# Fused attention block on one core: another order of stores and loads in stage one, and a separate path for the end of the last pair

## The reference

```python
h = _layernorm(x, axis=-1) * (1 + ca) + sa
x = x + ga * _L0_attn_ref(h, L0_attn_W_attn, L0_attn_W_proj)
h = _layernorm(x, axis=-1) * (1 + cb) + sb
x = x + gb * _L0_ffn_ref(h, ...)          # h @ W.T + b, and h @ (low-rank).T
```

## Time and profile before

| what | value |
|---|---|
| median of 3 runs | 1395.97 us (1394.33 to 1398.8) |
| the profiled execution, its own time | 1395.44 us |
| its span, first to last instruction | 1393.3 us |
| PE busy | 1251.6 us (90%) |
| ACT busy | 1274.1 us (91%) |
| DVE busy | 957.1 us (69%) |
| POOL busy | 194.4 us (14%) |
| last instruction of stage one on SP issued | 142.38 us |
| last exponential done | 1363.57 us |
| last computing instruction done | 1387.01 us |

### The profile page before, as it was taken

How to read it: one execution, slowest core, us unless ns; L and a number is a source line. 1 busy time by engine, 2 the same in 40 slices (tenths; PEclk the granted TensorE clock), 3 DMA queues, 4 the chain that set the end, 5 groups by cost and what they waited for, 6 DMA issues and landing times.

```text
span 1393.3 us, 28816 instructions
## 1 busy us (share of the span) xinstructions
PE 1251.6 (90%) x11067; PEld 742.9 (53%) x11067; DVE 957.1 (69%) x2082; ACT 1274.1 (91%) x2629; POOL 194.4 (14%) x405
## 2 busy tenths in 40 slices
PE   7994899999999999999999999999999988888784
PEld 5552455555555555555555555555555555444442
DVE  4852677777777777777777777777777766656453
ACT  2534899999999999999999999999999999999991
POOL 0323000201103030303011020303030201102030
PEclk9997899999999999999999999999999999999996
DMA  4795711010000001010101000000101010000000
GB/s 152 244 294 190 225 41 28 20 28 20 20 19 15 24 19 28 20 27 21 28 20 28 20 12 24 15 26 21 28 17 27 16 28 16 22 15 12 23 4 13
DMA packets 94447, 64.62 MB, mean 46 GB/s; under 512 B 59595, under 2 KB 89570, under 8 KB 94306
## 3 DMA queue, kind: packets, MB, share of 16 engines
q1 hardware_dynamic: 94306, 62.75, 15.2%
HBM read 41.74 MB, written 20.97 MB: 45 GB/s over the span
## 4 chain that ended last, share of the span: by engine, by line
PE 36%; ACT 34%; DVE 7%; issue 6%; ACTq 0%; DVEq 0%
ACT fast_s_ps L1087 21%; PE fast_s_ps L866 16%; ACT fast_probs L1087 12%; PE fast_t_ps L923 6%; PE fast_t_ps L892 5%; PE fast_t_ps L908 4%; DVE fast_negmax L1146 3%; PE fast_t_ps L954 2%; DVE fast_probsT L1165 2%; PE fast_s_ps L875 1%; PE fast_t_ps L934 1%; DVE fast_y_sb L1184 1%; DVE fast_probsT L1155 0%; PE fast_t_ps L967 0%; DVE fast_root_t L1247 0%
## 5 line engine op out<-in xcount | busy, mean ns | idle before, releaser
L1087 ACT ACTIVATE fast_s_ps<-fast_s_ps,fast_negmax 128x1024 f32<-128x1024 f32 (+4 forms) x768 | 853.8, 1152 | 3.3 <-PE fast_s_ps L866 2.8
L866 PE MATMUL fast_s_ps<-k_stack,xq 96*128 96x512 bf16 (+3 forms) x2448 | 664.6, 354 | 82.1 <-ACT fast_probs L1087 37.9
L1087 ACT ACTIVATE fast_probs<-fast_s_ps,fast_negmax 128x640 f32<-128x640 f32 (+7 forms) x512 | 496.3, 969 | 16.8 <-DVE fast_negmax L1146 16.7
L1146 DVE TENSOR_REDUCE fast_negmax<-fast_s_ps 128x1 f32<-128x512 f32 (+3 forms) x512 | 339.9, 664 | 111.7 <-PE fast_s_ps L875 109.6
L1155 DVE TENSOR_TENSOR fast_probsT<-fast_t_ps,fast_dec_c 128x384 f32<-128x384 f32 (+2 forms) x512 | 276.6, 540 | 182.0 <-PE fast_t_ps L892 179.5
L866 PEld LDWEIGHTS fast_s_ps<-k_stack,xq 96*128 96x128 bf16 x2448 | 202.3, 98 | 342.1 <-ACT fast_probs L1087 106.9
L892 PE MATMUL fast_t_ps<-ident,fast_probs 128*128 128x128 f32 x1488 | 249.6, 275 | 16.4 <-DVE fast_y_sb L1184 15.5
L1087 ACT ACTIVATION_READ_ACCUMULATOR fast_s_ps<-fast_s_ps,fast_negmax 128x1 f32 x768 | 259.6, 338 | 0.0
L892 PEld LDWEIGHTS fast_t_ps<-ident,fast_probs 128*128 128x128 f32 x1488 | 182.6, 141 | 64.0 <-DVE fast_y_sb L1184 22.6
L1165 DVE TENSOR_TENSOR fast_probsT<-fast_t_ps,fast_dec_c 128x256 f32<-128x256 f32 x464 | 192.1, 414 | 11.4 <-PE fast_t_ps L908 0.5
L908 PE MATMUL fast_t_ps<-ident,fast_probs 128*128 128x128 f32 x912 | 187.1, 285 | 7.8 <-DVE fast_probsT L1165 1.7
(11 more groups left out here) (119 smaller groups left out, 715.4 us busy)
## 6 DMA issues: line engine op xcount, KB each, us to landing
parts_d<-part SPq DMA_DIRECT2D x24, 512.0 KB, 4.4
k_stack<-parts_d SPq DMA_DIRECT2D x96, 128.0 KB, 2.9
xq<-parts_d SPq DMA_DIRECT2D x384, 32.0 KB, 2.1
fast_vals<-v_d SPq DMA_DIRECT2D x36, 128.0 KB, 2.5
xq<-x_dram SPq DMA_DIRECT2D x8, 512.0 KB, 6.5
v_d<-wa_t SPq DMA_DIRECT2D x8, 512.0 KB, 5.6
xb<-x_dram SPq DMA_DIRECT2D x32, 128.0 KB, 2.1
out_dram<-xb SPq DMA_DIRECT2D x32, 128.0 KB, 1.8
```

The source lines that it names most:

```text
L866: return nc.tensor.matmul(s_ps[:, n % SLOTS, at:at + w], q, k_stack[:, h, k0:k0 + w], start=True, stop=stop)
L1087: nc.scalar.activation(dst, src, ACT.Exp, bias=negmax[:, p % 2, side, h:h + 1], scale=-1.0, accum_out=sums[:, p % 2, side, h, c:c + 1]).th ...
L1146: nc.vector.tensor_reduce(out=negmax[:, p % 2, side, h:h + 1], in_=s_ps[:, n % SLOTS, CW - P * min(MAXW, b1 - b0):CW], axis=AX_X, op=ALU.m ...
```

## The change

It has four parts. First, in stage one SP issues the stores of mid and low ahead of `stack_keys(g - 1)`, which now comes at the end of the body of group g. Second, only the queries of the first 8 heads are loaded in stage one; those of the other 8 are loaded in stage two between the values of pair 0 and pair 1. Third, the last group is done in quarters: ACT makes each quarter of the high part from PSUM directly, DVE subtracts by quarters, ACT casts mid by quarters, POOL makes two quarters of low and DVE the other two; the low part of group 6 is made by DVE. Fourth, the end of the last pair has PSUM banks of its own in the ring of scores, one for each tile and step; ACT does the copies and a square root, and DVE takes the reciprocal; the turn of the last near tile waits for its own exponential alone; the sum of rows comes without the maximum for the check ahead of it. Besides, the preparation of the gates is spread over steps 7, 9 and 11, with the bias product in step 13 and the last weights in step 15.

```diff
-                    for n, ready in ((0, high_ready), (None, v_out), (1, mid_ready), (2, low_ready)):
-                        sp.wait_ge(ready, g + 1)
...
                         if n is None:
                             sp.dma_start(v_d[g], v_sb).then_inc(v_stored[b], 16)
-                            if 0 < g <= K_EARLY:
-                                stack_keys(sp, g - 1)
                             continue
...
                     body(g, g % 2, g // 2, min(g, 2), min(NG - 1 - g, 2))
+                    if 0 < g <= K_EARLY:
+                        stack_keys(sp, g - 1)
...
-                        for half in range(2):
-                            load_queries(sp, NT // 2, half, half, 0)
-                            load_queries(sp, NT // 2 - 1, half, half, 1)
+                        load_queries(sp, NT // 2, 0, 0, 0)
+                        load_queries(sp, NT // 2 - 1, 0, 0, 1)
...
+                def last_group(g, b, k):
...
+                    for m in range(4):
+                        act.wait_ge(kq_ready, g * 4 + (m + 1))
+                        nc.scalar.activation(kq32[:, b, m, :], kq_ps[:, m, :], ACT.Identity, bias=kq_bias[:, m:m + 1]
+                                             ).then_inc(kq_out, 1)
+                        if m == 0:
+                            act.wait_ge(part_stored[0][1 - b], (k + b) * 16)
+                        nc.scalar.activation(part[0][:, m, :], kq_ps[:, m, :], ACT.Identity, bias=kq_bias[:, m:m + 1]
+                                             ).then_inc(last_high, 1)
+                        if m == 1:
+                            act.wait_ge(part_stored[1][1 - b], (k + b) * 16)
+                        if m >= 1:
+                            middle(m - 1)
+                    middle(3)
...
-            WEIGHT_JOBS = {1: "down", 3: "up", 5: "both", 9: "bias"}
-            GATE_STEPS = (7, 11, 13)
+            WEIGHT_JOBS = {1: "down", 3: "up", 5: "both", 13: "bias"}
+            GATE_STEPS = (7, 9, 11, 13, 15)
...
                     load_vals(0)
+                    load_q(1)
                     load_vals(1)
...
-                    pe.wait_ge(exp_done, PER * NSTEP)
+                    pe.wait_ge(exp_done, PER * (NSTEP - 1) + order(LAST).index((NEAR, 0)) + 1)
                     turn(NEAR, NSTEP - 1)
...
+                    for side in (FAR, NEAR):
+                        pe.wait_ge(end_y_out, side + 1)
+                        for cc in range(CH):
+                            last = nc.tensor.matmul(end_p_ps[side][:, 0:C], tT[:, side, cc, :], wp_g[:, cc, :],
+                                                    start=(cc == 0), stop=(cc == CH - 1))
+                        last.then_inc(end_projected, 1)
...
+                    for side in (FAR, NEAR):
+                        pe.wait_ge(norm_ready, 2 * LAST + side + 1)
+                        for cc in range(CH):
+                            last = nc.tensor.transpose(end_t_ps[side][:, P * cc:P * (cc + 1)],
+                                                       y_sb[:, side, P * cc:P * (cc + 1)], ident[:])
+                        last.then_inc(end_n_turned, 1)
+                        pe.wait_ge(end_n_out, side + 1)
+                        dst = (t_ps[:, 0:C], tail_ps[:, 0:C])[side]
+                        for cc in range(CH):
+                            last = nc.tensor.matmul(dst, tT[:, side, cc, :], wf_g[:, cc, :],
+                                                    start=(cc == 0), stop=(cc == CH - 1))
+                        last.then_inc(end_linear, 1)
...
+                    nc.scalar.activation(sd2[:, 0:1], eps_t[:, 0:1], ACT.Sqrt, bias=eps_t[:, 0:1]).then_inc(sd_made, 1)
+                    for side in (FAR, NEAR):
+                        end_copy(side, end_y_turned, (tail_ps, end_n_ps[1])[side], end_y_out)
+                    act.wait_ge(sd_made, 1)
+                    for side in (FAR, NEAR):
+                        end_deviation(side)
+                        end_copy(side, end_n_turned, end_t_ps[side], end_n_out)
...
+                        x2 = xb[:, p % 2, side, :]
+                        serial(nc.vector.tensor_tensor(x2, x2, end_p_ps[side][:, 0:C], ALU.add))
+                        serial(nc.vector.bn_stats(q6[:, side, :], x2))
+                        nc.vector.bn_aggr(mv2[:, side, :], q6[:, side, :]).then_inc(end_stats, 1)
+                        dve.wait_ge(end_dev, side + 1)
+                        serial(nc.vector.reciprocal(rstd[:, side:side + 1], sd2[:, side:side + 1]))
+                        nc.vector.tensor_scalar(y_sb[:, side, :], x2, mv2[:, side, 0:1], rstd[:, side:side + 1],
                                                 ALU.subtract, ALU.mult).then_inc(norm_ready, 1)
```

166 lines of the change are left out of this document (112 added, 54 removed).

## The result

The changed kernel takes 1372.57 us (median of 4 runs, 1370.87 to 1372.86), the kernel before on the same chip 1397.38 (1394.33 to 1400.09): a ratio of 0.9819, 95% interval 0.9803 to 0.9835. The forecast was 1372, 23.5 us less; the medians on one chip are 24.8 apart. The profiled execution took 1372.60 us with a span of 1370.6; before it was 1393.3, so 22.7 us went.

| | before | after | change | forecast |
|---|---|---|---|---|
| start to first matmul of stage two | 142.97 | 134.47 | -8.5 | -15.0 |
| to the end of the last exponential | 1220.60 | 1217.47 | -3.1 | -0.9 |
| to the end of the last addition | 23.08 | 12.20 | -10.9 | -7.6 |
| to the end of the span | 6.65 | 6.46 | -0.2 | 0 |

A forecast was written before the change was run, and what follows sets the result against it. ACT bounds stage two, so gains lie in its waits and the two ends: 15.0 (stage one) + 0.9 (gates) + 7.6 (end) = 23.5 us off 1395.44 gives 1371.9, say 1372; range 1368 to 1380.

The forecast's parts named there:

- The groups: Stage one: storing low and mid ahead of the key loads spaces groups 12.6 us apart, making group 5 5.9 us earlier.
- T of group 5: Stage one: the end of POOL's subtraction for group 5, forecast at 105.2 us against 111.11 before.
- my 24.5: Stage one: least time for two groups, from low store, keys, issues, 4.4 us landing of high and 10.5 us cast-to-subtraction.
- The end of stage one: Last group in quarters with halved queries: stage one ends at 127.4 instead of 142.38, 15.0 us earlier including the groups.
- the 13.6 of the sum: Stage one: time from T of group 5 until group 6's high part has landed, giving 118.8 us.
- second rival: Last group of stage one: DVE and POOL block each other, DVE standing up to 2 x 1.0 us; 1374 us, chance 0.08.
- The first rival: Stage one: transfers are the bound at 13.9 us a group whatever the order; 1377 us, or 1379; chance 0.22.
- The gates: Stage two: spreading the gates' chain removes ACT's 1.49 us wait at step 7, at a price of 0.6: net 0.9 us.
- The end: Last exponential to last addition: the new chain takes 15.5 us in place of 23.1, 7.6 us less.
- Slower than before: Stage one: stores behind keys land so late (some 19 us) that groups wait for high; about 1400 us, chance 0.03.

The follow-up runs named there:

- another order: Changed kernel with three moves in SP's queue: x ahead of keys, next high store amid the keys, queries ahead of group 6's low store; 1372.28 us.
- fillers: Kernel with the old end of the last pair, plus unread matrix products issued on TensorE ahead of that end's jobs; 1384.26 us, ratio 0.9912.

## Why the prediction came out as it did

**The groups** (5.9 us, T of group 5 at 105.2) is a term that was mis-sized. The mechanism was right: the wait for x fell, low and mid no longer stand behind keys. The landing was not. I took 4.4 us from the old median for a store that now stands behind twelve loads. The high part of group 4 took 7.7 us, and groups 4 and 5 together 28.1 where my 24.5 has 4.4 in it. So from group 0 to group 5 it was 65.4 us where 62.7 were forecast: 2.7 us.

**The end of stage one** failed by another 1.6 us at the same start-up. The high part of group 6 landed 12.7 us behind T of group 5, better than the 13.6 of the sum. From there it took 9.6 us, not 8.2: 0.8 on ACT, which waited 0.71 us for the store of mid to land, a wait that the sum does not have, and 0.6 on DVE, where the last quarter cost 1.19 us beside POOL instead of 0.6. The last issue then ended 1.5 us after the last low part, not 0.4, behind a last high store that had waited 2 us for the queries, which I had seen end "just ahead" of it; in the two runs in which that store waits for nothing (half of the keys, and keys and queries, by GpSimd) it is 0.45. My second rival named the blocking of DVE and POOL and priced it at 2 us; it happened inside the forecast's path and cost 0.6 there. The rule of the exclusive lock in the Trainium skill ("SBUF — State Buffer", section on the two sides) holds for VectorE with two SBUF inputs, as the subtractions have, and agrees with POOL's 2.71 us for two quarters. The normalising (5.13 us in every group) has one tensor as input, so the rule as the prediction words it does not cover that figure.

**What the parts are worth** I had not asked. Undone one at a time, the halved queries give some 8 of stage one's 10.7 us, the order 1.0, hardly beyond the scatter, and the quarters nothing that can be told, because each ends in the same wait: the one high buffer, behind keys. With half of the keys on GpSimd the length is 89.5, where my terms add to 89.7 (127.4 and the 0.59 us from last issue to first matmul, less 38.25). That near-hit is in part luck. Its groups end at 104.4 (forecast 105.2) and high lands 12.7 us later (13.6), both better, and then it takes 9.6 us as well (8.2). What it does not have is the long landing in the groups and the last store behind queries. These two, 3.4 and 1.1 us at the same start-up, are the 4.5 us between the two kernels.

**The first rival**, transfers as the bound at 13.9 us a group, gave nearly the spacing measured (13.8 and 14.3), and is wrong as a cause: the same bytes went in 12.3 us a group with another order and with another issuer.

**The gates** (0.9): 1.49 us went and 0.29 came, 1.2 net; the price was half of my 0.6. The other 1.9 us of stage two lie within its scatter of 3.3 us between profiles of the same code, and I haven't traced them.

**The end** (7.6 us, measured 10.9). The chain was as forecast, the price of a product was not: I put all three products on the chain at the 2.07 us of half clock, and they came at 1.0, 1.13 and 1.13. That is 2.9 of the 3.3 us between 15.5 and 12.2, and the last transposes (0.44 for 0.65) are another 0.4. There is also a slip in the sum: its last step, two times 0.65 + 0.4 + 2.07 with 0.42 and 0.5, is 7.2 and not 6.7, so by its own terms the end was 16.0 us and the gain 7.1. The shorter chain goes with the full clock in all ten profiles, and where the root again took 1.8 us more on either side, the clock fell.

The errors were +4.2 us in stage one (and 2.2 of start-up, which is chance) against -3.3 in the end and -2.2 in stage two, of which the last can be scatter. The median hit 1372 because they cancel: that is luck, and of the three terms only the gates came near their price.

**Slower than before** did not come near: the longest landing of a part is 9.9 us where some 19 were needed, and none of the twelve kernels is slower than before. But its mechanism is what held up the late groups: two groups take 20.1 us plus the landing, by its formula, and with 7.7 that is 13.9 a group, where 13.8 and 14.3 were measured. The sum had 4.4 in that place.

## What to carry over

Where an engine waits for a DMA, look at what its queue was issuing when the data became ready: here a DMA share of 1.04 looked like a transfer limit and was one queue's order, and half of the key loads on GpSimd's idle time took 3.8 us more off by the medians (1368.75 us, and 1368.00 with all of them there). Undo each part of a change by itself, since parts that shift the same wait (a store order, a split into quarters) can be worth nothing together with one that does the work. At a sparse end, don't price the products by the old clock: a shorter chain can keep it up, and a longer one lose it.

## What was not expected of the hardware

- TensorE's clock fell in the end with the root on VectorE (one profile), after a stand of 3.10 us (0.86 in that window, 0.50 in the next), and not in the changed kernel, with stands of up to 1.33 us. But in the old end it had fallen to 0.75 in the six us from 1354 with stands of at most 1.24 us, and with fillers to 0.66 in a stretch in which it was busy for 4.75 of 5 us. No single stand explains all four, and what does is open. Nor does the work explain the start-up: one and the same matmuls ran at 1.00 between 24 and 34 us in eleven profiles and at 0.72 to 0.84 in three.
- Six key loads of 128 KB cost GpSimd 3.15 us to issue, 0.53 each, where SP takes 0.66 (7.89 for twelve), and the DMA engines then moved 330 GB/s at a share of 1.02 instead of 305 at 1.09.
- After many transfers issued by GpSimd the barrier at the end of the stage came later: 1.15 and 2.9 us behind SP's last issue with 60 and 72 loads, one profile each, and 0.4 with 30, as with none. Cause open.
- The start-up varies by 2 to 3 us between executions (POOL's first subtraction at 37.9 to 41.3), and the late ones are just those in which TensorE was granted less clock there. The first group's sixteen products for keys and queries took 7.13 us there in the kernel before and 8.83 in the changed kernel's profile.
